# Local attention on one core: the row maxima and their subtraction done per PSUM bank, and the keys' transposes in two groups of four with a wait each

## The chip, the cores and the metric

The kernel runs on one core of a Trainium2 chip. A core has five engines that run side by side and meet only at semaphores: TensorE (PE, with its weight loads listed apart as PEld), VectorE (DVE), ScalarE (ACT), GpSimd (POOL) and the queue engine SyncE (SP), which issues transfers. PE writes its results into PSUM, which has eight banks of 512 float32 columns by 128 partitions. The metric is the time of one launch on the device in microseconds, and less is better.

## The reference, cut to what matters

The program computes four pairs of branches over 2048 tokens of width 128. The change touches one of them, the second branch of the first pair: six layers, each made of attention inside windows of 32 tokens and a gated feed-forward part.

```python
# one of DEPTH = 6 layers; HEADS = 16, DIM_HEAD = 64, WINDOW = 32
q, k, v = jnp.split(x @ Wqkv, 3, -1)              # then split into heads
q = l2norm(q) * qs;  k = l2norm(k) * ksc
q = q * cos * scale + rotate_half(q) * sin * scale
k = k * cos * inv + rotate_half(k) * sin * inv
# a window of 32 queries sees its own 32 keys and the 32 before them
sim = jnp.einsum('bhwie,bhwje->bhwij', bq, bk2) * QK_SCALE
sim = jnp.where(mask, -jnp.finfo(sim.dtype).max, sim)
attn = jax.nn.softmax(sim, -1)                    # max, subtract, exp, sum, divide
out = jnp.einsum('bhwij,bhwje->bhwie', attn, bv2)
x = out_of_heads @ Wo                             # then the feed-forward part
```

## The kernel before

**Tiling.** The 2048 tokens are 16 blocks of 128 (`NB = 16`), so a layer has 16 blocks and the six layers have 96, numbered n = 0 to 95 straight through. The feed-forward part works on chunks of four blocks (512 tokens), 24 in all.

**A software pipeline of steps.** Every engine has its own `step(l, s, end)`, and all five walk s = 0, 1, 2, ... in the same order. In step s the kernel does, for different blocks at once: the projection to queries and keys of block s (`qk`, L972), their squares on ACT (L1202), the sums of these and the scaling on DVE (`norm` L1360 and L1366, `scale` L1372); the table products of block s on DVE (`table`, L1381) and the rotation on POOL (L1523, L1527); the transposes of block s-1 (`turn_q` L994, `turn_k` L1004) and its values (`vv`, L1013); the scores of block s-2 (`scores` L1031, L1036) and their softmax on DVE (`soft`, `inverse`, `probs`); the products of block s-3 with its values (`values`, L1058) and the output projection of block s-4 (`project`, L1075, added on DVE at L1412). From s = 8 on, the feed-forward part of earlier blocks is woven in: with j = (s-8) mod 4, steps of j = 1, 2, 3 hold one third of the up-projection each (`up`, L1095, two matmuls, the second behind the wait for `scale`), and steps of j = 0 hold the down-projection (`down`, L1103), its addition (L1436) and the layer norm (L1080, L1085, L1255 to L1268, L1416, L1420).

**Order.** Nothing is scheduled by a planner. Each engine does its instructions in the order in which they are written, and a wait at one of them holds all behind it on that engine. DVE's order in a step is: `norm` of block s, `soft` of s-2, `scale` of s, in steps of j = 0 the addition L1436 and the centring L1416, then `table`, `inverse` (L1393, L1395), `probs` (L1400, L1407), `add` (L1412). PE's order is: `qk`, first half of `scores`, `turn_q`, second half of `scores`, `vv`, `turn_k`, then `down` or the first `up` matmul, a wait for `scale` of this step (semaphore `lf_qn`, inside `values_ready`), the second `up` matmul, `values`, `project`, `values`.

**The two PSUM banks of the change.** Banks 4 and 5 are used in turn for the scores of block s-2 (eight heads in each bank), for the transposed keys of block s-1 (four transposes of 128 columns in each bank), and for single results later in the step. So `turn_k` may not write before `soft` has read the scores. In `soft`, one instruction takes the maxima of all 16 heads out of both banks (L1387, semaphore `lf_max`), and one subtracts them (L1389, semaphore `lf_sub`). `turn_k` waits for `lf_sub` ahead of its first transpose, ACT's exponential (`exps`, L1241) waits for it too, and ACT's copy of the transposed keys (`keep_k`, L1225, L1226) comes behind that exponential. Before `down` or the first `up` matmul, PE waits for `lf_v`, the end of ACT's copy of the values (`keep_v`, L1236).

Of the kernel before, what the change touches and what calls it, by code (L numbers as in the profile page):

```python
# [7 lines left out]
ALU = mybir.AluOpType  # L8
ACT = mybir.ActivationFunctionType
AX = mybir.AxisListType  # L10
# [3 lines left out]
P = 128  # L14
# [3 lines left out]
NB = T // P  # L18
# [44 lines left out]
def program(nc, d, out, stages=(0, 1, 2, 3), branches="af"):  # L63
# [3 lines left out]
    with ExitStack() as ctx:  # L67
# [8 lines left out]
        def S(name):  # L76

            if "_in" in name and name not in whole:
                whole[name] = ctx.enter_context(nc.semaphore(name))
            if name in whole:  # L80
                return whole[name]
            mine = named.setdefault(scope["branch"], {})
            if name not in mine:
                mine[name] = SHARED[len(mine)]
            return mine[name]
# [4 lines left out]
        PS = ctx.enter_context(nc.psum_tensor("banks", [P, 8, CH], F32))  # L90
# [96 lines left out]
        DEPTH, HEADS, DH, WIN = 6, 16, 64, 32  # L187
# [35 lines left out]
        lf_E = arena.f32_3(HEADS, 2 * WIN)  # L223
        lf_E2 = arena.f32_3(2 * HEADS, WIN)
        lf_PT = arena.f32_3(2 * HEADS, WIN)
        lf_st = arena.f32_3(2, HEADS)
# [732 lines left out]
        def lf_pe(pe):  # L959
# [38 lines left out]
            def turn_k(n, l):  # L998

                pe.wait_ge(S("lf_rotk"), l * NB + (n + 1))  # L1000
                if n >= 1:
                    pe.wait_ge(S("lf_sub"), l * NB + n)
                for p in range(8):
                    m = nc.tensor.transpose(PS[:, 4 + p // 4, p % 4 * P:(p % 4 + 1) * P], lf_ra[:, n % 2, INNER + p * P:INNER + (p + 1) * P], ident)  # L1004
                m.then_inc(S("lf_tk"), 1)

# [106 lines left out]
            def step(l, s, end):  # L1113
# [10 lines left out]
                if lf_live(s - 1, end):  # L1124
                    vv(s - 1, l)
                    turn_k(s - 1, l)

                    if ffn or ending:
                        pe.wait_ge(S("lf_v"), l * NB + s)
                elif s >= 1:  # L1130
                    ffn_taken(s - 1, l, end)
# [207 lines left out]
        def lf_dve(dve):  # L1339
# [43 lines left out]

            def soft(n, l):
                dve.wait_ge(S("lf_s"), l * NB + (n + 1))
                s = PS[:, 4:6].rearrange("p a (h k) -> p (a h) k", k=2 * WIN)
                nc.vector.tensor_reduce(lf_st[:, 0], s, AX.X, ALU.max).then_inc(S("lf_max"), 1)  # L1387
                dve.wait_ge(S("lf_max"), l * NB + (n + 1))
                nc.vector.tensor_tensor(lf_E, s, lf_st[:, 0].unsqueeze(2).broadcast_to([P, HEADS, 2 * WIN]), ALU.subtract).then_inc(S("lf_sub"), 1)  # L1389

            def inverse(n, l):
                dve.wait_ge(S("lf_exp"), l * NB + (n + 1))
# [46 lines left out]
            def step(l, s, end):  # L1439
                c, j, ffn = lf_chunk(s, end)  # L1440
                b, ending = lf_chunk_before(s, end)
                if ending:
                    product(b, 2, l)
                if ffn and j == 1:
                    normed(c, l)
                elif ffn and j >= 2:
                    product(c, j - 2, l)
                if lf_live(s, end):
                    norm(s, l)
                if lf_live(s - 2, end):  # L1450
                    soft(s - 2, l)
                if lf_live(s, end):
                    scale(s, l)
                if ending:
                    out_(b, l)
                if ffn and j == 0:
                    centre(c, l)
                if lf_live(s, end):
                    table(s, l)
                if lf_live(s - 2, end):  # L1460
                    inverse(s - 2, l)
                if lf_live(s - 2, end):
                    probs(s - 2, l, end)
                if lf_live(s - 4, end):
                    add(s - 4, l)
                if s == 0:
                    constants()
# [5 lines left out]
            def tail(l):  # L1473
                normed(2, l)
                soft(NB - 1, l)
                inverse(NB - 1, l)
                probs(NB - 1, l, True)
                add(NB - 3, l)
                product(2, 0, l, True)
                residual(0)  # L1480
                residual(1)
                add(NB - 2, l)
                product(2, 1, l, True)
                product(2, 2, l, True)
                add(NB - 1, l)
                centre(3, l, 2)
                out_(2, l, 3)
                normed(3, l)
                residual(2)
                product(3, 0, l, True)  # L1490
                product(3, 1, l, True)
                product(3, 2, l, True)
                out_(3, l, 5)
                residual(3)
# [688 lines left out]
        key, hi, top = slice(0, 64), slice(64, 96), slice(96, 128)  # L2183
# [1536 lines left out]
```

## Time and profile before

| | us |
|---|---|
| median of 3 runs (4059.45 to 4061.49) | 4060.26 |
| the profiled execution | 4064.39 |
| its span, first to last instruction | 4062.2 |
| the branch of the change, its first to its last score softmax (L1387) | 162.0 to 1816.2 |

So some 2 us of the profiled execution lie outside the span. The steps of the branch take about 41% of the span. How to read the rows further down: a line number is a line of the kernel before; "x8" is a count of instructions merged into one row; the number in brackets at a row's end is how long the engine sat idle before it, and the name behind it is the instruction that released it. Rows of PE are of matmuls, whose ends overlap the next start by some tens of nanoseconds.

### The profile page before, as it was taken

The page shows a single profiled execution, that of the slowest core. Times are in us where ns is not written, and L with a number is a line of the kernel's source. Part 1 is how long each engine was busy: PE and PEld are TensorE (multiplying, and loading weights), DVE is VectorE, ACT ScalarE, POOL GpSimd, SP SyncE. Part 2 cuts the span into 40 slices and gives each one's busy share as a digit, 9 for nine tenths or more (in the row PEclk, how much of TensorE's full clock was granted, in tenths as well). Part 3 has the DMA queues.
Part 4 walks back from the last instruction along what each step waited for, and adds up shares of the span by engine and source line. Part 5 has one row for each costly group of instructions (what it writes and reads, how often), then busy time and mean ns, then how long its engine had stood idle before and what let it go on. Part 6 is the DMA issues. An engine that isn't in the chain of part 4 may idle for free.

```text
span 4062.2 us, 121711 instructions
## 1 busy us (share of the span) xinstructions
PE 3684.0 (91%) x50424; PEld 2024.2 (50%) x50424; DVE 3048.9 (75%) x5108; ACT 2526.8 (62%) x3810; POOL 1248.0 (31%) x1096
## 2 busy tenths in 40 slices
PE   6799999999999999998999999999988699999998
PEld 2365555555555555555644555555554233333333
DVE  7788988888888989875637666667676777777772
ACT  6456666666666666665435555655564476767775
POOL 0466665656556655641100000000002011111121
PEclk8899999999999999997589999999999799999999
DMA  2123222223223222221000000000001211111100
GB/s 74 32 65 81 67 68 76 70 64 81 73 64 86 66 72 74 70 63 28 22 1 3 4 5 4 4 4 2 4 7 41 94 21 21 21 21 21 26 2 11
DMA packets 84727, 163.75 MB, mean 40 GB/s; under 512 B 26648, under 2 KB 36552, under 8 KB 82912
## 3 DMA queue, kind: packets, MB, share of 16 engines
q1 hardware_dynamic: 83937, 155.06, 14.6%
q8 instruction: 419, 6.86, 0.7%
q14 instruction: 148, 1.21, 0.1%
q10 hardware_dynamic: 223, 0.61, 0.1%
HBM read 40.88 MB, written 8.52 MB: 12 GB/s over the span
## 4 chain that ended last, share of the span: by engine, by line
PE 39%; issue 23%; POOL 18%; DVE 11%; ACT 6%; POOLq 0%; DMA 0%; DVEq 0%; SPq 0%; ACTq 0%
POOL arena L1523 9%; POOL arena L1527 7%; PE banks L1863 6%; PE banks L3162 5%; PE banks L1826 3%; ACT arena L3307 2%; PE banks L1844 2%; DVE arena L2033 2%; PE banks L3120 2%; PE banks L3136 2%; PE banks L1882 2%; POOL arena L1507 2%; DVE arena L2052 1%; DVE arena L3390 1%; DVE arena L1372 1%
## 5 line engine op out<-in xcount | busy, mean ns | idle before, releaser
L3390 DVE TENSOR_REDUCE arena<-banks 128x2 f32<-128x1024 f32 x512 | 613.9, 1223 | 198.5 <-PE banks L3127 93.3
L3307 ACT ACTIVATE arena<-banks 128x1024 f32<-128x1024 f32 x512 | 521.0, 1024 | 216.9 <-PE banks L3143 104.7
L1523 POOL TENSOR_TENSOR arena<-arena 128x512 f32<-128x512 f32 x384 | 424.7, 1127 | 638.2 <-DVE arena L1381 630.7
L1527 POOL TENSOR_TENSOR arena<-arena 128x1024 f32<-128x1024 f32 x192 | 533.1, 2776 | 15.1
L2033 DVE CUSTOM_DVE_ANT_0 arena<-arena,banks 128x512 f32<-128x512 f32 (+3 forms) x640 | 361.8, 603 | 145.1 <-issue 140.0
L972 PE MATMUL banks<-arena 128*128 128x512 f32 x768 | 370.4, 627 | 27.1 <-issue 14.5
L1971 ACT ACTIVATE arena<-banks 128x512 f32<-128x512 f32 (+3 forms) x320 | 168.7, 527 | 339.8 <-PE banks L1845 338.6
L3162 PE MATMUL banks<-arena 128*32 128x256 f32 x4096 | 335.1, 394 | 13.4 <-issue 8.3
L1963 ACT ACTIVATE arena<-arena 128x128 f32<-128x128 f32 (+15 forms) x256 | 328.6, 1285 | 14.0 <-DVE arena L2045 9.7
L1826 PE MATMUL banks<-arena 64*128 64x512 f32 (+3 forms) x1280 | 319.9, 575 | 6.4 <-issue 4.3
L2115 POOL COPY arena<-arena 128x512 f32<-128x512 f32 x32 | 19.7, 615 | 995.4 <-DVE arena L2059 995.4
L1360 DVE TENSOR_REDUCE arena<-arena 128x16 f32<-128x1024 f32 x192 | 229.9, 1215 | 108.2 <-ACT arena L1202 108.2
L2052 DVE COPY arena<-banks 128x512 f32<-128x512 f32 (+3 forms) x320 | 194.3, 607 | 139.8 <-PE banks L1844 139.4
L1844 PEld LDWEIGHTS banks<-consts,arena 64*128 64x128 f32 x2176 | 167.2, 139 | 219.3 <-issue 217.6
L1863 PE MATMUL banks<-arena 128*64 128x256 f32 (+1 forms) x2304 | 258.4, 374 | 0.4 <-issue 0.2
L1202 ACT ACTIVATE arena<-banks 128x1024 f32<-128x1024 f32 x192 | 194.6, 1023 | 101.8 <-PE banks L972 101.4
L1058 PEld LDWEIGHTS banks<-arena 64*64 64x64 f32 x12288 | 198.8, 135 | 109.4 <-issue 94.6
L1844 PE MATMUL banks<-consts,arena 64*128 64x64 f32 x2176 | 195.4, 227 | 60.1 <-DVE arena L2052 43.5
L1247 ACT ACTIVATE arena<-banks 128x1024 f32<-128x1024 f32 x96 | 99.6, 1037 | 215.9 <-PE banks L1058 215.9
L972 PEld LDWEIGHTS banks<-arena 128*128 128x128 f32 x768 | 143.8, 197 | 180.3 <-issue 155.5
L1058 PE MATMUL banks<-arena 64*64 64x32 f32 x12288 | 220.3, 221 | 11.9 <-DVE arena L1372 5.1
L1381 DVE TENSOR_TENSOR arena<-arena 128x1024 f32<-128x1024 f32 x192 | 226.7, 1223 | 2.6
(451 smaller groups left out, 7556.5 us busy)
## 6 DMA issues: line engine op xcount, KB each, us to landing
arena<-arena SPq DMA_DIRECT2D x768, 64.0 KB
arena<-arena SPq DMA_DIRECT2D x96, 384.0 KB, 3.6
arena<-arena SPq DMA_DIRECT2D x104, 128.0 KB, 3.4
arena<-in_lf_wqkv SPq DMA_DIRECT2D x6, 1024.0 KB, 5.3
arena<-arena SPq DMA_DIRECT2D x8, 512.0 KB
arena<-features_k SPq DMA_DIRECT2D x30, 128.0 KB
arena<-features_q SPq DMA_DIRECT2D x15, 216.0 KB
arena<-in_lf_wqkv SPq DMA_DIRECT2D x6, 512.0 KB, 4.0
```

The costliest lines, as they stand in the source:

```text
L972: m = nc.tensor.matmul(PS[:, j], lf_xb[:, n % 4], ck(lf_wqk, j), start=True, stop=True)
L1058: m = nc.tensor.matmul(PS[DH * h:DH * (h + 1), a, (2 * p + e) * WIN:(2 * p + e + 1) * WIN], vb[r, hd * DH:(hd + 1) * DH], lf_Z[r, e * HEAD ...
L1523: nc.gpsimd.tensor_tensor(r[:, :, e * H2:(e + 1) * H2], q[:, j, :, (1 - e) * H2:(2 - e) * H2], s[:, j, 1, e * H2:(e + 1) * H2].unsqueeze(1 ...
L1527: nc.gpsimd.tensor_tensor(a, a, lf_rb, ALU.add).then_inc(S("lf_rot" + x), 1)
L1826: m = nc.tensor.matmul(PS[:, 2 * h + u % 2, 0:n], at_q[p][r, t * P:(t + 1) * P], at_k[p][r, b * CH:b * CH + n], start=True, stop=True)
L1844: lower = nc.tensor.transpose(PS[:, 4, k * at_D:(k + 1) * at_D], ck(at_E[c % 2][x][h], 4 * b + j, P)[0:at_D], ident[0:at_D, 0:at_D])
L1863: m = nc.tensor.matmul(PS[h * at_D:(h + 1) * at_D, 6, x * 2 * P + o:(x + 1) * 2 * P], at_V[p][:, k, h * at_D:(h + 1) * at_D], at_PT[x][:, ...
L1963: nc.scalar.activation(e, e, ACT.Exp, bias=at_nm[c % 2][x][:, h:h + 1], scale=at_wo[at_par(c)][:, P + h:P + h + 1], accum_out=at_sum[c // ...
L2033: nc.vector.tensor_tensor_reduce(at_E[c % 2][x][h][:, b * CH:b * CH + n], at_dist[:, o:o + n], PS[:, 2 * h + u % 2, 0:n], 1.0, -3e38, ALU. ...
L3162: m = nc.tensor.matmul(PS[32 * c:32 * c + 32, 6, 256 * x:256 * x + 256], bi_v[p][:, h, k + y], bi_PT[(k + y) % 4][:, h * CH + 256 * x:h * ...
L3307: nc.scalar.activation(bi_PT[n % 4], PS[:, 2 * bi_slot("S", n):2 * bi_slot("S", n) + 2].rearrange("p a b -> p (a b)"), ACT.Exp).then_inc(S ...
L3390: nc.vector.tensor_reduce(bi_max[j % 2][:, t, :, c], PS[:, 2 * slot:2 * slot + 2], AX.X, ALU.max).then_inc(S("bi_mx"), 1)
```

## The change

`soft` becomes a loop over the two banks. For each bank: maxima of its eight heads, a wait for them, subtraction of these eight. The subtraction of bank 4 signals a new semaphore, `lf_sub_half`, and that of bank 5 the old `lf_sub`. `turn_k` waits for `lf_sub_half` ahead of its first four transposes, which write bank 4, and for `lf_sub` ahead of the other four, which write bank 5.

```diff
             def turn_k(n, l):
 
                 pe.wait_ge(S("lf_rotk"), l * NB + (n + 1))
-                if n >= 1:
-                    pe.wait_ge(S("lf_sub"), l * NB + n)
                 for p in range(8):
+                    if n >= 1 and p % 4 == 0:
+                        pe.wait_ge(S("lf_sub" if p else "lf_sub_half"), l * NB + n)
                     m = nc.tensor.transpose(PS[:, 4 + p // 4, p % 4 * P:(p % 4 + 1) * P], lf_ra[:, n % 2, INNER + p * P:INNER + (p + 1) * P], ident)
                 m.then_inc(S("lf_tk"), 1)
 
             def soft(n, l):
                 dve.wait_ge(S("lf_s"), l * NB + (n + 1))
-                s = PS[:, 4:6].rearrange("p a (h k) -> p (a h) k", k=2 * WIN)
-                nc.vector.tensor_reduce(lf_st[:, 0], s, AX.X, ALU.max).then_inc(S("lf_max"), 1)
-                dve.wait_ge(S("lf_max"), l * NB + (n + 1))
-                nc.vector.tensor_tensor(lf_E, s, lf_st[:, 0].unsqueeze(2).broadcast_to([P, HEADS, 2 * WIN]), ALU.subtract).then_inc(S("lf_sub"), 1)
+                for a, (top, sub) in enumerate((("lf_max_half", "lf_sub_half"), ("lf_max", "lf_sub"))):
+                    s = PS[:, 4 + a].rearrange("p (h k) -> p h k", k=2 * WIN)
+                    h = slice(8 * a, 8 * a + 8)
+                    nc.vector.tensor_reduce(lf_st[:, 0, h], s, AX.X, ALU.max).then_inc(S(top), 1)
+                    dve.wait_ge(S(top), l * NB + (n + 1))
+                    nc.vector.tensor_tensor(lf_E[:, h], s, lf_st[:, 0, h].unsqueeze(2).broadcast_to([P, 8, 2 * WIN]), ALU.subtract).then_inc(S(sub), 1)
```

On DVE, in a step of the layer loop, between `norm` and `scale` (names `sharedN` are semaphores: in before, shared25 is `lf_s` and shared53 is `lf_max`). Before:

```order
L1366 TENSOR_REDUCE arena<-arena 128x32 [waits shared41,shared43,shared44]
L1387 TENSOR_REDUCE arena<-banks 128x16 [waits shared25]
L1389 TENSOR_TENSOR arena<-banks,arena 128x1024 [waits shared53]
L1371 REGISTER_ALU [waits shared42]
L1372 TENSOR_TENSOR arena<-banks,arena 128x2048 [waits shared52]
```

The same place after the change, where line numbers and most semaphore numbers have moved (shared25 is `lf_s`, shared54 `lf_max_half`, shared55 `lf_max`):

```order
L1366 TENSOR_REDUCE arena<-arena 128x32 [waits shared42,shared44,shared45]
L1389 TENSOR_REDUCE arena<-banks 128x8 [waits shared25]
L1391 TENSOR_TENSOR arena<-banks,arena 128x512 [waits shared54]
L1389 TENSOR_REDUCE arena<-banks 128x8
L1391 TENSOR_TENSOR arena<-banks,arena 128x512 [waits shared55]
L1371 REGISTER_ALU [waits shared43]
L1372 TENSOR_TENSOR arena<-banks,arena 128x2048 [waits shared53]
```

Two instructions over 16 heads have become four over 8, two of them behind a wait for the one just ahead; nothing else of DVE's order has moved. On PE, in a step of j = 3, from `turn_k` to the second `up` matmul (shared26 is `lf_rotk`, shared21 is `lf_sub`, shared1 is `lf_h`, shared17, 2 and 5 are the waits of `values_ready`, shared17 being `lf_qn`). Before:

```order
L1004 MATMUL banks<-consts,arena 128x128 [waits shared26,shared21]
L1004 MATMUL banks<-consts,arena 128x128 x7
L1095 MATMUL banks<-arena 85x512 [waits shared1]
L1044 REGISTER_ALU
L1047 REGISTER_ALU [waits shared17]
L1048 REGISTER_ALU [waits shared2]
L1095 MATMUL banks<-arena 85x512 [waits shared5]
```

After the change (here shared21 is `lf_sub_half` and shared27 is `lf_sub`):

```order
L1004 MATMUL banks<-consts,arena 128x128 [waits shared26,shared21]
L1004 MATMUL banks<-consts,arena 128x128 x3
L1004 MATMUL banks<-consts,arena 128x128 [waits shared27]
L1004 MATMUL banks<-consts,arena 128x128 x3
L1095 MATMUL banks<-arena 85x512 [waits shared1]
L1044 REGISTER_ALU
L1047 REGISTER_ALU [waits shared17]
L1048 REGISTER_ALU [waits shared2]
L1095 MATMUL banks<-arena 85x512 [waits shared5]
```

The wait for the whole subtraction has moved from the first to the fifth transpose, and what follows the transposes waits as before.

## Rows read from the trace of the kernel before

**Rows 1.** Busy time by engine, 260 to 1800 us: PE, PEld, DVE, ACT, POOL, granted clock.

```profile
260.00:1800.00 1540.00, 1429.24 (x27565) 893.45 (x27569) 1351.08 (x1272) 1038.67 (x1466) 937.90 (x615) 0.99 0.27 71
```

**Rows 2.** Who waited for whom, 150 to 1845 us: us in total, times, longest.

```profile
PE banks L1004 <- DVE arena L1389: 54.1, 93, 0.9
...
DVE arena L1387 <- PE banks L1036: 25.1, 57, 3.7
...
PE banks L1095 <- DVE arena L1372: 18.7, 66, 0.4
```

**Rows 3.** Timeline of DVE, a step of j = 2 into j = 3: start, length.

```profile
784.15 1.23 DVE L1387 TENSOR_REDUCE arena<-banks 128x16 f32<-128x1024 f32 x1 [0.41 <-PE banks L1036]
785.41 1.23 DVE L1389 TENSOR_TENSOR arena<-banks,arena 128x1024 f32<-128x1024 f32 x1
786.55 2.28 DVE L1372 TENSOR_TENSOR arena<-banks,arena 128x2048 f32<-128x2048 f32 x1
...
800.62 1.23 DVE L1387 TENSOR_REDUCE arena<-banks 128x16 f32<-128x1024 f32 x1 [0.29 <-PE banks L1036]
```

**Rows 4.** Timeline of PE, the same stretch.

```profile
786.79 1.06 PE L1004 MATMUL banks<-consts,arena 128*128 128x128 f32 x8 [0.61 <-DVE arena L1389]
787.69 1.02 PE L1095 MATMUL banks<-arena 128*128 128x512 f32 x2
788.89 1.13 PE L1095 MATMUL banks<-arena 128*128 128x512 f32 x2 [0.18 <-DVE arena L1372]
...
791.01 2.05 PE L1075 MATMUL banks<-arena 128*128 128x128 f32 x16
...
799.72 0.86 PE L1036 MATMUL banks<-arena 64*32 64x64 f32 x64
```

**Rows 5.** Timeline of DVE, from j = 3 through j = 0 to j = 1.

```profile
803.02 2.28 DVE L1372 TENSOR_TENSOR arena<-banks,arena 128x2048 f32<-128x2048 f32 x1
...
823.87 0.75 DVE L1436 SCALAR_TENSOR_TENSOR arena<-banks,arena 128x512 f32<-128x512 f32 x1 [1.64 <-PE banks L1103]
...
838.60 2.28 DVE L1372 TENSOR_TENSOR arena<-banks,arena 128x2048 f32<-128x2048 f32 x1
```

**Rows 6.** Timeline of ACT in that step of j = 0.

```profile
812.67 0.63 ACT L1255 ACTIVATE arena<-arena 64x512 f32<-64x512 f32 x1 [0.33 <-DVE arena L1412]
...
817.23 1.09 ACT L1219 ACTIVATE arena<-banks 128x512 f32<-128x512 f32 x2
...
819.90 1.02 ACT L1236 ACTIVATE arena<-banks 128x1024 f32<-128x1024 f32 x1 [0.98 <-PE banks L1013]
```

**Rows 7.** Timeline of PE in that step of j = 0.

```profile
820.18 1.06 PE L1004 MATMUL banks<-consts,arena 128*128 128x128 f32 x8 [0.31 <-DVE arena L1389]
821.08 2.75 PE L1103 MATMUL banks<-arena 128*128 128x512 f32 x6
```

**Rows 8.** Timeline of PE and ACT, the step of j = 0 at a layer boundary.

```profile
612.76 1.06 PE L1004 MATMUL banks<-consts,arena 128*128 128x128 f32 x8 [0.48 <-DVE arena L1389]
613.66 2.75 PE L1103 MATMUL banks<-arena 128*128 128x512 f32 x6
...
612.40 1.02 ACT L1236 ACTIVATE arena<-banks 128x1024 f32<-128x1024 f32 x1 [1.06 <-PE banks L1013]
```

**Rows 9.** Groups of instructions by line: busy us, mean ns, idle before.

```profile
L1366 DVE TENSOR_REDUCE arena<-arena 128x32 f32<-128x64 f32 x96 | 21.3, 222 | 3.8
...
L1416 DVE TENSOR_TENSOR arena<-arena,banks 128x512 f32<-128x512 f32 x24 | 16.5, 688 | 6.2 <-PE banks L1080 4.3
```

**Rows 10.** Timeline of PE in step 5, and the window 210 to 220 us.

```profile
210.36 1.07 PE L1004 MATMUL banks<-consts,arena 128*128 128x128 f32 x8 [0.82 <-DVE arena L1389]
212.46 1.46 PE L1058 MATMUL banks<-arena 64*64 64x32 f32 x64 [1.04 <-DVE arena L1372]
213.85 3.30 PE L1075 MATMUL banks<-arena 128*128 128x128 f32 x16
...
210.00:220.00 10.00, 8.60 (x157) 7.21 (x158) 9.44 (x9) 4.39 (x7) 5.04 (x3) 0.83 0.22 62
```

## What the change does to the time: the prediction

> **What bounds the kernel now.** I first read the busy times of the stretch of the branch, without its first steps and its last [rows 1]. In 1540 us PE is busy for 1429 (93%), DVE for 1351 (88%), ACT for 1039, POOL for 938. No engine is full, two are nearly so, and such shares do not say which one a change must relieve. The next view is who waited for whom [rows 2]. PE stands idle before `turn_k` (L1004) until the subtraction L1389 is done, 93 times and 54.1 us in all, 0.58 us each. This is the wait that the change aims at. But PE also waits for `scale` (L1372) at the second `up` matmul (L1095), and DVE waits for PE's scores before the maxima (L1387), 57 times. A wait is worth something only if what follows it is not held by a later one, so the timelines of one step decide.
>
> **A step of j = 2 or 3** [rows 3, 4]. DVE takes the maxima at 784.15, subtracts at 785.41, scales at 786.55 and is done at 788.83. PE's transposes start at 786.79, after 0.61 us of waiting; the first `up` matmul starts at 787.69; then PE waits 0.18 us for the scaling, and starts the second one at 788.89. From there to the end of the scores at 800.58 PE has no wait. At 800.62 DVE takes the next maxima, after 0.29 us of idling for these scores. So the loop that closes is: scaling, PE's row of work to the end of the scores, maxima, subtraction, scaling. `soft` lies in it with its full length. The transposes do not: they are followed by a wait for the scaling, which ends later.
>
> **Steps of j = 0 and j = 1** [rows 5 to 7]. From the scaling of the j = 3 step (803.02) DVE works through to its addition L1412, which releases ACT's L1255 at 812.67. ACT then goes on to the copies of the queries (L1219, 817.23), which release PE's `vv`, which releases the copy of the values (L1236, 819.90 to 820.92), behind which the down-projection starts at 821.08. DVE meanwhile has done its softmax part and its scaling and waits 1.64 us for that down-projection before L1436. So in j = 0 `soft` has a cover of 1.64 us. After L1436 DVE has no wait up to the scaling of the j = 1 step at 838.60, so there `soft` counts in full again.
>
> **The change part by part.**
>
> *Length of a half.* DVE reads 1024 elements per partition in 1.23 us (L1389) and 2048 in 2.28 us (L1372) [rows 3], 1.03 ns each with 0.17 us fixed: 0.70 us for 512. The subtraction of 512 elements out of PSUM in L1416 took 0.688 us, and a reduction of only 64 took 0.222 us, which against 1.23 for 1024 gives 1.05 ns each and 0.69 us for 512 [rows 9]. I take 0.69. An instruction that waits for the one ahead starts 0.03 us after its end (784.15 + 1.23 = 785.38, start 785.41), and one that does not starts 0.09 us before it (785.41 + 1.23 = 786.64, start 786.55) [rows 3].
>
> *Cost on DVE.* Before, from the start of the maxima to the start of the scaling: 1.26 + 1.14 = 2.40 us. After: two pairs, each 0.69 + 0.03 and then 0.69 - 0.09, so 2 x 1.32 = 2.64; with the third decimals of the same rows (0.034 and 0.087) 2.65. The difference is 0.25 us per step. With halves of 0.68 or 0.70 us it is 0.21 or 0.29. These are the bounds; I stay at 0.25 since L1416 is the same engine, source and size.
>
> *Effect on `turn_k`.* The subtraction of bank 4 is done 0.72 + 0.69 = 1.41 us after the maxima start, 785.56 in the step above, before `vv` has left PE (786.79 - 0.61 = 786.18). So the first four transposes start where `vv` ends and wait for nothing. The other four wait for the second subtraction, which ends 0.25 us later than the old one. Eight transposes hold PE for 0.90 us (786.79 to 787.69), four for 0.45. PE leaves `turn_k` 0.45 - 0.25 = 0.20 us earlier than before. In j = 1, 2, 3 this is given to the wait for the scaling, which grows by 0.45. It is worth nothing there.
>
> *Steps of j = 0.* The down-projection waits for the transposes and for L1236. In the clean step the transposes would let it start at 821.08 and L1236 at about 821.06: nothing to gain. At a layer boundary [rows 8] L1236 ends at 613.42, so the down-projection could start near 613.56 and not at 613.66: 0.1 us, at four boundaries 0.4 us, and 0.02 us at each of the others, another 0.3 at most.
>
> *What hides the rest.* ACT's exponential waits for the second subtraction, 0.25 us later; in rows 3 and 4's step it is queued behind L1236, which follows `vv` by a full 1.0 us, later than the subtraction. If that cover were gone, `keep_k` would come 0.25 us later, and the projection that reads it stands more than 2 us behind. Nothing that DVE or PE do sits on SP's or POOL's queue; both receive their work 0.25 us later, with the loop. The added wait on PE holds only transposes and what follows, which waits for the scaling anyhow.
>
> *The sum.* `soft` runs 96 times. Of them 66 are in steps from 9 to 95 that are not j = 0, 6 in steps 2 to 7, where PE waits for the scaling too (1.04 us in step 5 [rows 10]), and I add 3 for step 8 and the two of the end, where the next thing also stands behind it: 75 x 0.25 = 18.8 us. The other 21 have the cover of 1.64 us. Less 0.7 for j = 0: **18 us**. Against the profiled execution that is 4064.4 + 18 = 4082.4; that execution was 4.1 us above the median of the runs, so I carry the difference over to the median: 4060.3 + 18 = **4078.3 us**, 0.44% slower.
>
> **The rivals.**
>
> *The wait of `turn_k` is what counts (faster).* If in most steps what follows the transposes ran on at once, each of the 93 waits would give 0.20 us: 18.6 us, 4041.7 us. It decides in any step where the scaling ends before PE has left the first `up` matmul. For it: 54.1 us of waits there. Against it: the wait for the scaling behind it, at L1095 66 times [rows 2, 4]. The Trainium skill, page "Perfetto Trace Analysis", section "Optimizing Scalar/DVE Operations", says that where DVE is not saturated but causes bubbles on other engines, breaking up instructions may let work complete sooner; this rival is that rule at work. The trace speaks against it here, since the bubble moves to the next wait. 5%.
>
> *Only the steps in which DVE is full pay (no change).* If in j = 2 and 3 the time came out of DVE's own idle time, only j = 1 (22 steps), the first 7 and the last 2 would pay: 31 x 0.25 = 7.8 us, 4067.6 us after the 0.4 of the boundaries. For it: DVE idles there before L1387. Against it: that idling lies ahead of `soft`, which is held by PE, and PE by the scaling. 5%.
>
> *The clock (much slower).* In step 5 PE waits 0.82 us and 1.04 us around `turn_k`, and just behind that the granted clock falls: 0.83 on the mean of that window, `project` (L1075) takes 3.30 us and not 2.05 [rows 4, 10]: 1.25 us on the path, and with the end of `values`, where the fall begins, an estimated 1.5. Half speed is the lower of the clock's two levels. The change makes PE's waits longer, 0.79 to 1.04 us in rows 3 and 4's step, still well short of the 1.86 of step 5. If the j = 1 steps, whose wait at L1004 is the longest (0.9 us [rows 2]), fell too: 22 x 1.5 = 33 us on top, 4111 us. 5%. If only steps 2 to 4 fell like step 5: 5 us, within my range.
>
> **How the numbers follow.** Forecast (all steps but j = 0 pay 0.25 us): 85%, its own range 4070 to 4088 (0.21 to 0.29 us a step gives 15 to 21 us; 5 us more for the clock in the first steps, 5 less if the ends and first steps hide it). Rivals 5% each. The range for 8 in 10 I put at 4068 to 4090. A measurement of this kernel can tell about 0.2%, 8 us. Faster by more: 5%. Within it: the second rival and the forecast's low end, 7%. Slower: 88%.
>
> **What would show it.** Four instructions of about 0.69 us in `soft`, 2.65 us from the first to the scaling, and no longer gaps between them. L1004 in two groups, the first with next to no wait, the second with 0.5 us or less. The wait for the scaling at the second `up` matmul 0.4 to 0.5 us longer. Steps of j = 1, 2, 3 longer by 0.25 us, steps of j = 0 (from soft to soft of j = 1, where DVE's 1.64 us shrinks to 1.4) as before. DVE's wait for the scores before the maxima stays. The forecast is wrong if halves take 0.62 us or less, if the second `up` matmul no longer waits, or if the clock falls in steps where it held.

## The result and the profile after

The changed kernel took 4075.86 us (median of 12 runs, 4067.43 to 4083.82) against 4060.64 us before (12 runs, 4053.71 to 4070.94). The ratio is 1.0035, with an interval of 1.0024 to 1.0046: 15 us slower, 10 to 19. The range on record was 4068 to 4090 and the likeliest value 4078.3. The profiled execution after has a span of 4073.8 us, 11.6 more than before; the one of before was itself some 4 us above its median, so the median is the better measure of the total and the traces the better measure of a step.

DVE after the change, the softmax part and the scaling of a step of j = 2 (start, length, tile; the answer to [rows 3]):

```profile
785.98 0.69 DVE L1389 TENSOR_REDUCE arena<-banks 128x8 f32<-128x512 f32 x1 [0.42 <-PE banks L1036]
786.70 0.69 DVE L1391 TENSOR_TENSOR arena<-banks,arena 128x512 f32<-128x512 f32 x1
787.31 0.68 DVE L1389 TENSOR_REDUCE arena<-banks 128x8 f32<-128x512 f32 x1
788.03 0.69 DVE L1391 TENSOR_TENSOR arena<-banks,arena 128x512 f32<-128x512 f32 x1
788.64 2.28 DVE L1372 TENSOR_TENSOR arena<-banks,arena 128x2048 f32<-128x2048 f32 x1
```

From the first maxima to the scaling it is 788.64 - 785.98 = 2.66 us, against 2.40 before. From one scaling to the next in that stretch, j = 2 to j = 3, it is 805.36 - 788.64 = 16.72 us, against 803.02 - 786.55 = 16.47. The softmax part still starts on the end of PE's scores.

PE in the same stretch, to be laid beside [rows 4]:

```profile
787.83 0.60 PE L1004 MATMUL banks<-consts,arena 128*128 128x128 f32 x4
788.78 0.66 PE L1004 MATMUL banks<-consts,arena 128*128 128x128 f32 x4 [0.35 <-DVE arena L1391]
789.27 1.02 PE L1095 MATMUL banks<-arena 128*128 128x512 f32 x2
790.97 1.13 PE L1095 MATMUL banks<-arena 128*128 128x512 f32 x2 [0.68 <-DVE arena L1372]
```

The first four transposes wait for nothing, the other four 0.35 us. Counted from the maxima, PE reaches the first `up` matmul 3.29 us later (789.27 - 785.98), before 3.54 us (787.69 - 784.15). Then it waits 0.68 us for the scaling and not 0.18, and the second `up` matmul comes 4.99 us after the maxima and not 4.74. PE gained a quarter of a microsecond and lost it again, and another quarter with it, within two instructions.

Who waited for whom, over all steps (total us, times, longest), answering to [rows 2]:

```profile
PE banks L1095 <- DVE arena L1372: 48.8, 66, 0.8
...
PE banks L1004 <- DVE arena L1391: 15.9, 57, 0.6
...
PE banks L1004 <- POOL arena L1529: 7.6, 23, 0.9
```

The wait of the transposes for the subtraction fell from 54.1 to 15.9 us, that for the scaling rose from 18.7 to 48.8. The last row is new in its size: 23 times, in every step of j = 1 and in one more near the start, the first four transposes now stand behind POOL's rotation of the keys, the other thing they need; in the steps of j = 1 this wait is some 0.3 us (before, such waits were two, 2.7 us in all).

The step of j = 0, answering to [rows 5, 7]. PE:

```profile
820.22 1.98 PE L1013 MATMUL banks<-arena 128*128 128x512 f32 x4 [0.64 <-ACT arena L1219]
822.04 1.29 PE L1004 MATMUL banks<-consts,arena 128*128 128x128 f32 x8
823.32 1.13 PE L1103 MATMUL banks<-arena 128*128 128x512 f32 x2
```

DVE:

```profile
826.21 0.75 DVE L1438 SCALAR_TENSOR_TENSOR arena<-banks,arena 128x512 f32<-128x512 f32 x1 [1.39 <-PE banks L1103]
```

(The row of L1103 is cut at the window's end: it is the first two of six matmuls.) DVE's wait for the down-projection has shrunk from 1.64 to 1.39 us: the 0.25 us of this step are paid out of it.

**A table for all kernels.** For each kernel I took the starts of the scaling in all 96 steps from DVE's timeline and, from step 8 on, the median distance between two of them, by the j of the step that ends the distance. It leaves out what differs from one execution to the next at layer boundaries.

| kernel | j = 0 | j = 1 | j = 2 | j = 3 | sum |
|---|---|---|---|---|---|
| before | 16.95 | 18.66 | 16.75 | 16.46 | 68.82 |
| changed | 17.20 | 18.66 | 17.00 | 16.72 | 69.58 |
| e1, split, whole wait | 17.19 | 18.91 | 17.00 | 16.72 | 69.82 |
| e2, maxima first | 16.95 | 18.65 | 16.74 | 16.46 | 68.80 |
| e7, maxima first, whole wait | 16.94 | 18.66 | 16.73 | 16.46 | 68.79 |
| e6, quarters | 17.70 | 19.42 | 17.50 | 17.23 | 71.85 |
| e3, before with late wait | 16.95 | 18.66 | 16.52 | 16.14 | 68.27 |
| e4, changed with late wait | 17.21 | 18.66 | 16.90 | 15.77 | 68.54 |
| e5, maxima first, late wait | 16.95 | 18.66 | 16.60 | 15.56 | 67.77 |

A distance that ends in j holds the softmax part of that step, and the way to it from the step before. The change adds 0.25, 0.00, 0.25 and 0.26: three steps in four pay it, 0.76 us per four steps.

### The profile page after: what moved, and what is told of

The parts are those of the page before. It is cut to its first block, busy times and chain, and to the rows that moved or that the text cites. A ratio compares the mean times of both kernels' runs of the same rounds, so it can differ in the third digit from the quotient of the medians.

```text
span 4073.8 us, 121903 instructions
## 1 busy us (share of the span) xinstructions
PE 3694.6 (91%) x50424; PEld 2028.8 (50%) x50424; DVE 3070.5 (75%) x5300; ACT 2526.8 (62%) x3810; POOL 1248.0 (31%) x1096
## 3 DMA queue, kind: packets, MB, share of 16 engines
q14 instruction: 139, 1.14, 0.1%
## 4 chain that ended last, share of the span: by engine, by line
PE 42%; issue 22%; POOL 15%; DVE 12%; ACT 7%; DMA 0%; POOLq 0%; DVEq 0%; SPq 0%; ACTq 0%
POOL arena L1525 8%; PE banks L1865 6%; POOL arena L1529 6%; PE banks L3164 5%; PE banks L1828 3%; ACT arena L3309 2%; PE banks L972 2%; PE banks L1846 2%; DVE arena L2035 2%; PE banks L3122 2%; PE banks L3138 2%; DVE arena L1372 2%; PE banks L1884 2%; DVE arena L2054 1%; PE banks L1058 1%
## 5 line engine op out<-in xcount | busy, mean ns | idle before, releaser
L972 PE MATMUL banks<-arena 128*128 128x512 f32 x768 | 367.7, 623 | 27.4 <-issue 14.3
L1058 PEld LDWEIGHTS banks<-arena 64*64 64x64 f32 x12288 | 200.4, 136 | 108.5 <-issue 91.5
L972 PEld LDWEIGHTS banks<-arena 128*128 128x128 f32 x768 | 143.1, 196 | 179.0 <-issue 154.2
L1058 PE MATMUL banks<-arena 64*64 64x32 f32 x12288 | 221.9, 222 | 10.8 <-DVE arena L1372 7.3
```

Source lines behind the costliest of these rows:

```text
L972: m = nc.tensor.matmul(PS[:, j], lf_xb[:, n % 4], ck(lf_wqk, j), start=True, stop=True)
L1058: m = nc.tensor.matmul(PS[DH * h:DH * (h + 1), a, (2 * p + e) * WIN:(2 * p + e + 1) * WIN], vb[r, hd * DH:(hd + 1) * DH], lf_Z[r, e * HEAD ...
```

## Experiments

The theory: `soft` lies with its whole length on the loop of scaling, PE's work, scores, softmax, scaling, and the early transposes are held by the wait for the scaling. The rivals: the wait of the transposes counts, or the cost is partly hidden. Each ratio below is to runs of the kernel before taken beside the experiment: median 4060.17 us (29 runs) for e1 to e4, 4056.36 us (23 runs) for e5 to e7.

**e1: the split alone.** From the changed kernel:

```diff
-                for p in range(8):
-                    if n >= 1 and p % 4 == 0:
-                        pe.wait_ge(S("lf_sub" if p else "lf_sub_half"), l * NB + n)
+                if n >= 1:
+                    pe.wait_ge(S("lf_sub"), l * NB + n)
+                for p in range(8):
```

> DVE's four half instructions as in the changed kernel, but PE waits for the whole subtraction ahead of its first transpose, as before. Theory (only the length of the softmax part on DVE counts, the early transposes give nothing that is kept but 0.7 us in steps of j = 0): the same time as the changed kernel within 2 us, so 15 to 18 us over the kernel before. Rival (the early transposes earn part of their 0.45 us back, and hide a larger cost of the halves): 0.45 us x 66 steps = 30 us more than the changed kernel, 45 us over the kernel before.

Measured: 4078.61 us (5 runs), ratio to before 1.0043 (1.0030 to 1.0056), 17 us slower, 12 to 23. The rival's 45 us are out, and j = 2 and 3 are those of the changed kernel, 17.00 and 16.72: there the early transposes are worth nothing. But the profile shows what this expectation missed. In j = 0:

```profile
756.71 1.98 PE L1013 MATMUL banks<-arena 128*128 128x512 f32 x4 [0.68 <-ACT arena L1219]
759.26 1.06 PE L1004 MATMUL banks<-consts,arena 128*128 128x128 f32 x8 [0.57 <-DVE arena L1391]
760.16 2.75 PE L1103 MATMUL banks<-arena 128*128 128x512 f32 x6
```

From the start of `vv` to the down-projection it is 3.45 us, in the changed kernel 823.32 - 820.22 = 3.10, before (821.08 - 817.88) 3.20. With the whole wait the split costs 0.25 us in this step too, and the distance ending in j = 1 goes to 18.91. So the early half of the transposes does one useful thing: it keeps the cost of the split out of j = 0. That is seen in the steps only; 22 x 0.25 = 5.5 us between 17 and 15 us of extra time is less than the two intervals can tell apart.

**e2: the same four instructions, maxima first.** From the changed kernel:

```diff
-                for a, (top, sub) in enumerate((("lf_max_half", "lf_sub_half"), ("lf_max", "lf_sub"))):
-                    s = PS[:, 4 + a].rearrange("p (h k) -> p h k", k=2 * WIN)
-                    h = slice(8 * a, 8 * a + 8)
-                    nc.vector.tensor_reduce(lf_st[:, 0, h], s, AX.X, ALU.max).then_inc(S(top), 1)
+                s = [PS[:, 4 + a].rearrange("p (h k) -> p h k", k=2 * WIN) for a in range(2)]
+                h = [slice(8 * a, 8 * a + 8) for a in range(2)]
+                for a, top in enumerate(("lf_max_half", "lf_max")):
+                    nc.vector.tensor_reduce(lf_st[:, 0, h[a]], s[a], AX.X, ALU.max).then_inc(S(top), 1)
+                for a, (top, sub) in enumerate((("lf_max_half", "lf_sub_half"), ("lf_max", "lf_sub"))):
                     dve.wait_ge(S(top), l * NB + (n + 1))
...
```

> The same four instructions in another order: both maxima, then both subtractions, so that no instruction waits for the one right ahead of it; the transposes in two groups as in the changed kernel. Theory (the 0.25 us come from two more fixed parts, of which only the write-out of a half that the next must wait for is exposed): an instruction that does not wait starts 0.60 us after the one ahead, so 4 x 0.60 = 2.40 us from the first maxima to the scaling, as with two whole instructions: no change against the kernel before, within 3 us. Rival (each extra instruction costs its fixed part whatever the order): 0.25 us a step again, 15 to 18 us over the kernel before.

Measured: 4056.04 us (12 runs), ratio 0.9990 (0.9981 to 1.0000): no change, or up to 8 us faster. The four sums of the table are those of before. DVE's timeline:

```profile
1107.86 1.28 DVE L1389 TENSOR_REDUCE arena<-banks 128x8 f32<-128x512 f32 x2
1109.06 1.28 DVE L1392 TENSOR_TENSOR arena<-banks,arena 128x512 f32<-128x512 f32 x2
1110.26 2.28 DVE L1372 TENSOR_TENSOR arena<-banks,arena 128x2048 f32<-128x2048 f32 x1
```

From the first maxima to the scaling it is 2.40 us, with four instructions as with two, and 0.26 us less than with the same four in the order of the change. That it is just the 2.40 us of before is a balance. From the start of a half to the start of the next instruction it is 0.60 us here, and 0.72 us in the changed kernel where the next one waits for it; over the whole 16 heads, before, it was 1.14 us without such a wait and 1.26 us with it [rows 3]. So each extra instruction costs 2 x 0.60 - 1.14 = 0.06 us, two of them 0.12, and each wait for the instruction just ahead costs 0.12. The kernel before has one such wait, the changed kernel two, e2 none: the 0.25 us of the change are 0.12 for the number of instructions and 0.12 for the second wait, and e2 pays the first by having no wait at all.

**e7: maxima first, and the transposes behind the whole subtraction.** The edit of e1 made in e2.

> Both maxima, then both subtractions, and PE's transposes behind the whole subtraction as before. Theory (the early transposes are worth nothing where DVE's part is not longer): the time of the same order with transposes in two groups, 4056 us, within 4 us. Rival (the early transposes are what kept that kernel at the time of before): 10 us or more above it.

Measured: 4058.15 us (12 runs), ratio 1.0002 (0.9990 to 1.0015). The intervals of e2 and e7 overlap and their steps are alike to 0.01 us. Where DVE's part is no longer than before, the two groups of transposes give nothing that can be measured.

**e6: a larger dose.** Four pairs over four heads each, PE behind all of them. From e1 (the six lines of its loop give way to seven, of which three are shown; one signal to PE comes at the end of the last quarter):

```diff
-                for a, (top, sub) in enumerate((("lf_max_half", "lf_sub_half"), ("lf_max", "lf_sub"))):
+                for a in range(4):
+                    s = PS[:, 4 + a // 2, a % 2 * 256:(a % 2 + 1) * 256].rearrange("p (h k) -> p h k", k=2 * WIN)
+                    h = slice(4 * a, 4 * a + 4)
...
```

> The softmax part of DVE in four pairs of maxima and subtraction over four heads each, each subtraction behind its own maxima; PE waits for all of it, as before. A quarter is 256 elements: about 0.42 us by the slope and fixed part of the halves. A pair takes 0.42 + 0.03 + 0.42 - 0.09 = 0.78 us, four 3.1 us against 2.40: 0.7 us a step. Theory (every step but j = 0 pays it, and j = 0 too since the transposes wait for all of it and the down-projection for them): (75 + 22) x 0.7 = 68 us over the kernel before. Rival (the cost is on the path only in part of the steps, or as much again hides in DVE's idle time): under 40 us.

Measured: 4137.86 us (5 runs), ratio 1.0194 (1.0175 to 1.0212): 79 us slower, 71 to 86. Quarters of DVE, each 0.42 to 0.43 us long:

```profile
1104.57 0.43 DVE L1389 TENSOR_REDUCE arena<-banks 128x4 f32<-128x256 f32 x1 [0.28 <-PE banks L1036]
...
1107.74 2.28 DVE L1372 TENSOR_TENSOR arena<-banks,arena 128x2048 f32<-128x2048 f32 x1
```

The part is 1107.74 - 1104.57 = 3.17 us long, 0.77 more than before, and all four distances of the table are longer by 0.75 to 0.77. With 0.77 in the place of the 0.7 that I had expected, and 96 steps (my 97 counted one too many), 96 x 0.77 = 74 us, inside the interval. So three times the cost of the change is paid in full too; nothing in DVE's idle time takes it up, not even in j = 0, where the down-projection now comes later as well.

**e3 and e4: the wait behind the transposes taken away.** The scaling reads banks 0 to 3; the second `up` matmul writes bank 7 and doesn't need it. In e3 (from before) and e4 (from the changed kernel) PE waits after it. Nobody waits for `lf_masking`: its increment gives the waits an instruction of their own to stand at, and is one instruction more for PE in each step:

```diff
-                if lf_live(s - 3, end):
-                    values_ready(s - 3, l, end)
                 if ffn and j:
                     up(c, j - 1, l, 1)
-                elif ffn:
+                if lf_live(s - 3, end):
+                    values_ready(s - 3, l, end)
+                    pe.sem_inc(S("lf_masking"), 1)
+                if ffn and j == 0:
                     mean(c, l)
```

> The kernel before, with PE's wait for the scaling moved from ahead of the second up matmul to behind it, ahead of the products with the values that need it. Theory (the wait behind the transposes is what holds PE in steps of j = 1, 2, 3): PE's 0.35, 0.18 and 0.35 us of idling there go; those of j = 1 and 2 are on the loop, that of j = 3 is not since the next step hangs on DVE: 22 x 0.53 = 12 us less than the kernel before (8 to 19). Rival (the wait of the transposes alone counts, the later one is hidden): no change.

> The changed kernel with the same late wait. Theory: now the transposes are the last thing that holds PE, so leaving them 0.20 us earlier counts in j = 1 and 2, and 0.25 us of DVE counts only once in four steps: the change is then worth -0.40 + 0.25 = -0.15 us per four steps, 22 x -0.15 = -3 us against the kernel before with the late wait, where it was +15 without. So some 15 us under the kernel before. Rival (the cost on DVE counts wherever PE waits): again 15 us over the kernel before with the late wait.

Measured: e3 4058.14 us (11 runs), ratio 0.9997 (0.9988 to 1.0006); e4 4062.91 us (12 runs), ratio 1.0006 (0.9995 to 1.0017). Both expectations missed in size, e4 also in sign; the 15 us that e4's rival put between the two kernels did not come either. In the steps e3 did what was expected: 0.23 and 0.32 us less in j = 2 and 3, 0.55 per four steps, 12 us over 22 groups. But of these 12 us at most 5 are in the time. And with the late wait the change costs 0.27 us per four steps (68.54 - 68.27) where it cost 0.76 without; in the medians 5 us instead of 15, though the intervals of e3 and e4 overlap. So the wait for the scaling is shown to be what held the early transposes: with it gone, j = 3 got 0.37 us shorter through the change (16.14 to 15.77), where it had got 0.26 longer. But j = 2 got 0.38 us longer (16.52 to 16.90).

Part of what ate the rest is in PE's rows of e4. "Issue" marks a gap that nothing in the profile released:

```profile
1098.37 0.43 PE L1036 MATMUL banks<-arena 64*32 64x64 f32 x26
1099.50 0.63 PE L1036 MATMUL banks<-arena 64*32 64x64 f32 x38 [0.70 <-issue]
```

Gaps like this cut the small score matmuls in two. All such gaps of PE's matmuls in the branch, summed over its timeline, add up to 22 us before, 32 us in e3 and 51 us in e4. Of each sum some 14.5 us are the four gaps before the projection (L972) at the layer boundaries, alike in all three. What a gap costs depends on the step. Of the distances ending in j = 2 in e4, the three without a gap in L1036 or L1058 are 15.98 to 16.26 us and the fourteen with over 0.4 us of gap 16.83 to 17.25: there the gaps go with the longer time, and the three are no longer than the ten of e3 without a gap (16.11 to 16.36). Of those ending in j = 0, eleven have a gap of 0.2 to 0.9 us in L1036 and still take 17.2 us, as without one: there it is hidden.

Another part may be TensorE's clock. Its mean over a run is 0.950 in the median of e3's and of e4's runs, against 0.952 in the runs of before beside them, and 0.949 against 0.953 in e5. At one of two levels, full or half, 0.002 of 4060 us is 16 us more at half speed, so by estimate up to 8 us of PE's time in e3 and e4 and up to 16 us in e5, less what falls into PE's waits. No run here separates this from the gaps.

**e5: maxima first with the late wait.** e2 with the edit of e3, the best that these parts could make.

> Maxima first, then subtractions, transposes in two groups, and PE's wait for the scaling behind the second up matmul. DVE's part costs nothing here (its order alone gave the times of before) and PE leaves the transposes up to 0.45 us earlier, with no wait behind them. Theory without a further limit: 0.75 us per four steps under the kernel before with the late wait alone, 22 x 0.75 = 16 us, some 4042 us. Rival, from the run of the changed kernel with the late wait, where gaps of 0.5 to 0.9 us in front of the small score matmuls came up that nothing released: PE's supply of instructions takes the gain back, steps of j = 2 stay at 16.9 us, and the time is that of the kernel before within 6 us.

Measured: 4053.10 us (12 runs), ratio 0.9994 (0.9981 to 1.0007): the time of before, as the rival had it. The steps are neither's: j = 2 is 16.60 us and not the rival's 16.9, and the gain on e3 is 68.27 - 67.77 = 0.50 us per four steps and not 0.75. Against before they are faster by 68.82 - 67.77 = 1.05 us per four, 23 us over 22 groups. Some of this is lost once per pass of the layer loop, four steps behind its start (steps 16, 32, 48, 64 and 80):

```profile
672.09 0.43 PE L1058 MATMUL banks<-arena 64*64 64x32 f32 x15 [3.57 <-issue]
672.46 5.38 PE L972 MATMUL banks<-arena 128*128 128x512 f32 x8
```

The same gap is 0.91 us before, at 672.97, and the projection behind it, 3.70 us elsewhere, takes 5.38 here: after the 3.57 us of idling it runs in part at the lower clock (0.76 on the mean of 673 to 680 us, 1.00 there before), as it does after the gap at a layer boundary. The five distances with this gap are together 15.6 us above the median for j = 0, in the trace of before 4.5 us; so some 11 of the 23 us are found here. Between single traces, which differ by several us anyway, the rest can't be placed. So no kernel here is shown to be faster than the one before. e2 is the nearest, its interval ends at 1.0000.

## Why the prediction was right, point by point

**What bounds the steps.** Right. The place of `soft` on the loop is shown by e6, where 0.77 us of DVE is 0.75 to 0.77 us of every step, and by the changed kernel's own distances.

**The length of a half.** 0.69 us predicted; 0.686 us for the maxima and 0.693 us for the subtraction measured, in the means over 192 each. The part is 2.66 us long, 2.64 to 2.65 predicted. e2 adds what it is made of: half of it is two more instructions, half a second wait for the instruction just ahead, and another order of the same four takes all of it back.

**`turn_k`.** The first group without a wait, the second with 0.35 us, PE out of it 0.25 us earlier (0.20 predicted), and the wait for the scaling longer by 0.50 us in the step shown (0.45 predicted). In steps of j = 1 the first group doesn't start where `vv` ends, as I had it for all steps, but waits some 0.3 us for POOL's rotation, which I had not looked at; the wait for the scaling hides this too. That leaving the transposes early is worth nothing where that wait stands is shown by e1 beside the changed kernel (j = 2 and 3 alike) and by e4 beside e3 (worth something once it is gone).

**Steps of j = 0.** The cover of 1.64 us held and shrank to 1.39. The reasoning was thin in one point: I priced the early transposes at 0.7 us in all there. They are worth 0.25 us in each such step of a kernel that has the split, as e1 shows. Against the kernel before they are worth nothing: the down-projection starts 3.10 us behind `vv` and not 3.20, but the distance ending in j = 1 is 18.66 us in both, so what I took off for it in ordinary steps is not seen, and the 0.4 us at the layer boundaries are too little to be seen. The cover, too, has two parts. I named only DVE's wait of 1.64 us; e1 has that wait and pays all the same. It also takes what I had worked out for `turn_k` and not named here: PE leaves it no later than before, so the down-projection doesn't move. The sum was right because it charged j = 0 with nothing.

**The sum.** 75 x 0.25 = 18.8 us less 0.7, 18 in all; measured 15, 10 to 19. By the table, 22 x 0.76 = 17 us in the steps of the feed-forward part. The first steps pay as well, as I had it: of the seven distances that end in steps 2 to 8, six are longer by 1.6 us in all, and the seventh has the fall of the clock in the execution before. The profiled pair shows less, 10.5 us from the first scaling to the last, because single steps differ between executions whatever the kernel: the boundary step 44 took 23.04 us in the execution before and 22.15 in the one after, against 22.06 and 22.08 for step 28.

**The rivals.** That the wait at the transposes counts: out as a description of this kernel, partly right as one of e4's, in j = 3. That only j = 1 pays: out. By the table the distances ending in j = 2 and 3 are longer by 0.25 and 0.26 us; the one ending in j = 1 isn't longer, since it begins with DVE's shrunken wait in j = 0 and so gives back what j = 1 costs. The clock: it didn't fall more often, nine times from the first scaling to the last against ten before. In step 5, where it had fallen before [rows 10], it held, with a longer wait:

```profile
210.99 1.14 PE L1058 MATMUL banks<-arena 64*64 64x32 f32 x64 [1.54 <-DVE arena L1372]
212.06 2.05 PE L1075 MATMUL banks<-arena 128*128 128x128 f32 x16
```

The mean granted clock of the span is 0.952 in both. I had put the wait's length forward as what brings the fall about; by this row it is not that alone.

## What to carry to other kernels

Before splitting an instruction so that a waiting engine can start earlier, look at what that engine waits for next: a wait behind the one removed takes the whole gain, while the splitting engine pays at once if it is on the loop. If a split is wanted, put the halves that do not depend on each other side by side; here that took the cost from 0.26 us a step to nothing. And a wait removed from a busy TensorE has to be followed through the whole loop: here gaps that nothing released, and a lower mean clock, came with it, and the time stayed.

## What was not expected of the hardware

TensorE's gaps without a releaser grew in the three kernels with the late wait: 22 us in the branch before, 32 in e3, 43 in e5, 51 in e4. They stand in the stretches of the smallest matmuls (L1036, 64 columns, and L1058, 32 columns) and once per pass of the layer loop, where a gap of at most 1.6 us before is 2.3 to 3.6 us in e4 and e5. It looks as if TensorE's instructions arrive no faster than it works through such stretches, and as if its waits had served to let them catch up. That is only argued, and e2 speaks against its simplest form: there TensorE's waits for other engines fell from 114 to 94 us, below e3's 98, and the gaps stayed at 22. The late wait also gives TensorE one more instruction a step and puts its waits elsewhere in the step, and no run here has one without the other. What sets these gaps stays open.
